# A hand-written order of steps: lead-in apart from the steady pairs, output rows scattered by halves of ranks, codes' buffers given back at the one-hots

## The reference

```python
# layer 0
h = relu(layernorm(x)); x = x + (adj / clip(adj.sum(2), 1)) @ h
# layer 1, on h = relu(layernorm(x))
neigh = (adj_ > 0) & ~eye                     # adj_: adj with ones on the diagonal
rank = cumsum(neigh) - neigh; nb = neigh.sum(-1)
skip = where(nb > 10, (nb + 1) // 2, 1)
rem = neigh & (skip > 1) & (rank % skip == skip - 1) & mask
rem = rem | rem.T; nd = where(rem, 0, adj_) > 0
s = sort(where(nd, h, inf)); nv = nd.sum(2)   # over the neighbours, for each channel
agg = sum(w * interpolate(s, tau * (nv - 1)) for tau, w in ((.25, .25), (.5, .5), (.75, .25)))
x = x + (relu((h + agg) @ W1 + b1) @ W2 + b2) * mask
```

## Time and profile before

| | us |
|---|---|
| median of 3 runs | 1654.02 |
| lowest and highest | 1653.05, 1656.76 |
| profiled execution, own time | 1666.68 |
| its span in the trace | 1664.6 |

### The profile page before, as it was taken

One profiled execution on the slowest core, in us unless ns is written; L12 is line 12 of the kernel. 1 busy time (PEld: TensorE's weight loads), 2 busy tenths in 40 slices (PEclk: granted clock), 3 DMA queues, 4 the chain that ended last, 5 costly groups with the idle time before them and its releaser, 6 DMA issues. The chain is left out here.

```text
span 1664.6 us, 29516 instructions
## 1 busy us (share of the span) xinstructions
PE 1270.5 (76%) x10929; PEld 847.7 (51%) x10929; DVE 1375.1 (83%) x2557; ACT 1227.5 (74%) x2099; POOL 775.7 (47%) x996
## 2 busy tenths in 40 slices
PE   4675897879888788878888788869888797768642
PEld 3553664556546564556546464556546564444320
DVE  3444459999899898989899898989899898969990
ACT  3687797988788797968788788868788787833310
POOL 0252425271628643383728643383616744631344
PEclk9966598999898898979898998979798898979775
DMA  5464754463536362554536363454526462330100
GB/s 157 139 208 133 235 189 138 149 205 118 171 106 219 113 219 88 172 167 136 182 104 220 112 216 94 163 164 131 197 82 224 124 210 67 109 82 23 30 12 13
DMA packets 139386, 233.99 MB, mean 141 GB/s; under 512 B 62910, under 2 KB 63438, under 8 KB 139224
## 3 DMA queue, kind: packets, MB, share of 16 engines
q1 hardware_dynamic: 124888, 185.54, 36.4%
q0 software_dynamic: 14336, 46.42, 7.4%
HBM read 181.31 MB, written 50.59 MB: 139 GB/s over the span
## 5 line engine op out<-in xcount | busy, mean ns | idle before, releaser
L560 PE MATMUL psG<-OHB,HL 128*64 128x384 f16 (+5 forms) x3584 | 387.4, 361 | 55.1 <-DVE OHB L1065 34.8
L1045 DVE TENSOR_TENSOR_SCAN VR<-NEI 128x1024 f16<-128x1024 f16 x128 | 296.8, 2336 | 125.0 <-POOL NEI L1270 57.3
L481 PE MATMUL psL<-H0A,ADJT 128*128 128x65 f32 x2048 | 311.9, 311 | 65.1 <-DMA ADJT<-in_adjt 37.3
L481 PEld LDWEIGHTS psL<-H0A,ADJT 128*128 128x128 f32 x2048 | 294.7, 224 | 101.7 <-DMA ADJT<-in_adjt 61.2
L560 PEld LDWEIGHTS psG<-OHB,HL 128*64 128x64 f16 x3584 | 213.0, 117 | 195.7 <-DVE OHB L1065 54.0
L1270 POOL TENSOR_TENSOR NEI<-NEI,CH 128x128 f16<-128x128 f16 x128 | 114.1, 894 | 295.8 <-ACT NEI L743 294.5
L1328 POOL DMA_INDIRECT rows<-VR,IDX x128 | 185.4, 1449 | 57.9 <-ACT NEI L779 34.4
L774 ACT ACTIVATE VR<-psT,CF 128x512 f16<-128x512 f32 x256 | 168.5, 681 | 24.6 <-PE psT L511 22.4
L1132 DVE TENSOR_TENSOR HUB<-HUB 128x1472 f32<-128x1472 f32 (+6 forms) x224 | 178.4, 796 | 8.1 <-ACT HUB L884 7.9
L1133 DVE TENSOR_TENSOR HUB<-HUB 128x1472 f32<-128x1472 f32 (+6 forms) x224 | 184.8, 825 | 0.0
L1362 POOL DMA_INDIRECT out<-FR x128 | 162.1, 1266 | 37.5 <-issue 36.9
(11 more groups left out here) (120 smaller groups left out, 2260.9 us busy)
## 6 DMA issues: line engine op xcount, KB each, us to landing
ADJ<-in_adj SPq DMA_DIRECT2D x128, 512.0 KB
...
RR<-rows SPq DMA_DIRECT2D x128, 288.0 KB
...
rows<-VR,IDX POOLq DMA_INDIRECT x128
out<-FR POOLq DMA_INDIRECT x128
```

The source lines that it names most:

```text
L481: m = e.matmul(ps["L"][:, 65 * (t % 4):65 * (t % 4) + 65], ADJT[:, hf, j, :], H0A[:, T * b + k, :], start=(k == 0), stop=(k == T - 1), ski ...
L560: m = e.matmul(bk[C * b:C * b + C, 0:cols], HL[:, part, (2 * g + b) % 3, k, :], OHB[:, n % 2, b, kk * cols:kk * cols + cols], start=(k == ...
L1045: e.tensor_tensor_scan(VR[:, t, 0:N], NEI[:, t, 2:N + 2], NEI[:, t, 1:N + 1], 0.0, ALU.add, ALU.add).then_inc(v_cum, 1)
```

## The change

1. The string ORDER is another one of the same letters, and the lead-in, up to the first full period, is written out in a string of its own, LEAD_IN. SKEW and LEAD go; LATE says by how many places six strands start later. The steps are the same ones, each as often; their order differs a little on every engine.
2. `out` is cut otherwise: not one graph's eight tiles after both additions, but four tiles of either graph after the addition of their half (`put`).
3. ACT's copy into POSA or POSB waits until the last one-hots of the block that used the buffer are made (DVE), instead of until they are gathered (PE).

```diff
@@ -22,19 +22,18 @@
 BIG = 1.0e9
 NOMATCH = 9999.0
 COLS = 512
-LEAD = 4
-
 
 ORDER = (
-    "mRJAssMtQQcNtfJtsQdtFMJtmQtQtdtANetdtQNQQQkmmMMQQdSdQQmQSQaQQmQQcQeLdAMMsFcmssQfQSFSALMdQcDDLMsesSAcdRmS"
-    "FMMAVessMMDDTmcSAsQEsDcEdhVSmvFKDMMKdABEBKvdBBmMDMDTdKeFEmRBmeoBEKErBldmrgNFBdKLdrrmFEmrNdeekmdmKdedXEmr"
-    "NrrmeLnQKFstnscssFKAnMsFtMcSsKLFtLScSssdAMtQsscDMdtsDcsSFEAtmMSLMcsAsMSdMEDtEcssSRcSFFADmMMFFtQTtLdFALMM"
-    "FmmAeLQFDFQLtdOMMBFFAmFFDBDQQtLdMLFeFmhBrDrFQTMtQtrlBLFFFQQetQrLdBBBBdrtgrrrGOQtmmFsJsGtdctQJsset")
-
-SKEW = {
-    "A": 24, "B": 24, "D": 24, "E": -11, "F": 13, "G": 0, "J": -3, "K": 0, "L": 7, "M": 48, "N": 6, "O": -2,
-    "Q": -24, "R": 5, "S": 16, "T": 6, "V": 0, "X": 2, "a": -1, "c": 17, "d": 3, "e": 1, "f": 0, "g": 3,
-    "h": 2, "k": 2, "l": 2, "m": 2, "n": 6, "o": 0, "r": 24, "s": 36, "t": -10, "v": 0}
+    "rrtLmJmfQFetJQsstcdJssRtmAssQQNtMJtcFdtJsMmtQtQAtdtNtdtVeQQQkMmQmQQMNQQQcdQmQedQQmdSQQQSSdAMsLFcmSQaMQfs"
+    "AMFDsLMecssDDAmdseSQhcRSFMMsmEAVDLcMTEsMAdEsSBcmKlvDFMMSKAdFDKdDDvmrTMdBBMRtFerEmBKgBBedmmBBKEELdLdemNFK"
+    "rEXmedkNmodrmrdrEmKdFFLrNermsenKsnscsscKntFsKcAtLdMsSMstssSQEcFsDtSAmcdFStMLMsscSEAMsDdMAtMDsscMFSFSmDAT"
+    "cSQERMFFMtQLtAFMDFBMmdLemFLFQQtFOFAMMDdmLAFFBQQLLtdDDBtFFTmLehFQMQrtlFrFQQtBFQteOddBgBBBtGMQrGrrr")
+LEAD_IN = (
+    "XAnnnMMAMMDDAMMADMMADRMMDTAMMBBADMrMrADDMBMTBBrBRrBrBgNrrrNsscssAsscMcNssMAkMMSScAMSMssSAMDDssccMsSSRADD"
+    "TMsMAssMcDDcMSASMMADDThBBBrrBMMlBRgBBNBXNkNnrrrrrrsnssscssccnAMMssAcMMSSsDsLAMsMScsASsDsScchMMsDSsRSDcST"
+    "AMMAMMADFLFMBBFMLFDALFFrLMBFFrBFDLDlFTFFBBBBdrdMrrrg")
+
+LATE = {"E": 11, "J": 5, "O": 2, "Q": 25, "a": 1, "t": 13}
 
 
 
@@ -136,7 +135,7 @@
 
 def strands():
 
-    s = {c: [] for c in SKEW}
+    s = {c: [] for c in ORDER}
 
     def add(c, kind, *args):
         s[c].append((kind, *args))
@@ -202,8 +201,8 @@
         for ch in range(2):
             add("E", "yt", g, ch)
             add("E", "mk", g, ch)
-        for b in range(2):
-            add("O", "out", g, b)
+        for ch in range(2):
+            add("O", "out", g, ch)
 
     for g in range(NP):
         add("X", "lx", g)
@@ -233,11 +232,12 @@
 
 def plan():
 
+
     pl = Plan()
     pl.do("start")
     steps = strands()
-    at = {c: SKEW[c] - LEAD * len(steps[c]) // NP for c in SKEW}
-    for c in ORDER * (NP + 2 * LEAD):
+    at = {c: 0 if c in LEAD_IN else -LATE.get(c, 0) for c in steps}
+    for c in LEAD_IN + ORDER * (NP + 2):
         if 0 <= at[c] < len(steps[c]):
             kind, *a = steps[c][at[c]]
             if kind in ("pos", "turn", "dg", "sc", "nvt", "nvr", "flg", "f1", "f2"):
@@ -383,6 +383,9 @@
 
             return sum(1 for s in steps[:steps.index(step)] if s[0] == kind)
 
+
+        MADE = {(g, blk): 1 + max(nth["gd", g, c, 1] for c in OF[blk]) for g in range(NP) for blk in OF}
+        LAST = {"b1": (1, "b2a"), "hub": (1, "b2b"), "b2a": (0, "b1"), "b2b": (0, "hub")}
         GATHERED = {(g, blk): 1 + max(nth["gm", g, c, 1] for c in OF[blk]) for g in range(NP) for blk in OF}
         ROWED = {g: 1 + max(nth[s] for s in steps if s[0] == "cr" and s[1] == g) for g in range(NP)}
         SUMMED = {(s[1], s[2]): 1 + i for i, s in enumerate(s for s in steps if s[0] == "wz" and s[2] != "hub")}
@@ -783,10 +786,10 @@
                 u = t_use("pos", g, b, rt)
                 blk, = [n for n, (_, r0, width) in BLOCKS.items() if r0 <= rt * P < r0 + width]
                 area, r0, _ = BLOCKS[blk]
-                before = {"b1": (g - 1, "b2a"), "hub": (g - 1, "b2b"), "b2a": (g, "b1"), "b2b": (g, "hub")}[blk]
+                back, last = LAST[blk]
                 w.wait_ge(t_full, u + 1)
-                if before[0] >= 0:
-                    w.wait_ge(p_gm, GATHERED[before])
+                if g >= back:
+                    w.wait_ge(v_oh, MADE[g - back, last])
                 e.activation(POS[area][:, b, :, rt * P - r0:rt * P - r0 + P],
                              t_bank(u).bitcast(F16).rearrange("p (k n) -> p k n", n=P), ACT.Copy).then_inc(t_empty, 1)
 
@@ -1354,10 +1357,10 @@
                 e.tensor_tensor(x1, x1, HID[:, ch, :].rearrange("p (t b c) -> p b t c", b=2, c=C), ALU.add).then_inc(
                     o_fin, 1)
 
-            def put(g, b):
-                fr = FR[:, (2 * g + b) % 4]
-                w.wait_ge(o_fin, 2 * (g + 1))
-                for rt in range(T):
+            def put(g, ch):
+                w.wait_ge(o_fin, 2 * g + ch + 1)
+                for b, rt in itertools.product(range(2), range(4 * ch, 4 * ch + 4)):
+                    fr = FR[:, (2 * g + b) % 4]
                     dst = fr[:, rt, R_DST - R_X1:R_DST - R_X1 + 2].bitcast(I32)
                     e.indirect_dma_start(out_d, bass.IndirectOffsetOnAxis(ap=dst, axis=0),
                                          fr[:, rt, 0:2 * C].bitcast(F32), None).then_inc(d_out[g % 2], 16)
```

## The result

The changed kernel takes 1704.65 us (median of four runs, 1698.42 to 1711.24) against 1654.18 us: a ratio of 1.0303, 95% interval 1.0258 to 1.0349. It is 50 us slower where 9 us faster was forecast. Run once more, beside the experiments, it gave 1.0279 (1.0222 to 1.0335). Its profiled execution reports 1711.24 us.

A forecast was written before the change was run, and what follows sets the result against it. DVE sets the pace and only its idle time, about 16 us a pair, can be won. Terms -20.1 - 5.0 - 3.8 - 4.2 + 3.0 + 21.0 = -9.1 took 1654.0 to 1645 us; range 1626 to 1666.

The forecast's parts named there:

- A: Valid-neighbour count dgv earlier on POOL: PE's 4.80 us wait and DVE's one-hot wait at chunk 7 go; -20.1 us.
- B: First half of output scatters one mask earlier on POOL: count waits of 6.5 become 0.3 and 4.4 to 6.1; -5 us.
- C: Merge step 17: its copy on ACT no longer stands behind other work; 0.95 us in four pairs, -3.8 us.
- E: adj(4,0,0) later on ACT, behind two more codes, delaying the scatter cnt(4,0,0) awaits; +3.0 us in six pairs.
- F: Short DVE waits like one of 0.69 us vanish when DVE itself comes later; -0.7 in six pairs, -4.2 us.
- D: FR's load ahead of adj(4,1,0) on SP: late ADJ tile makes DVE's merge step 20 wait 4.2 us; +21 us.
- the two other edits: Output scatters by halves, and codes' buffers freed at the one-hots instead of the gathers: both forecast at 0.
- Third rival: Slower: FR's load is late and POOL doesn't run ahead, merge step 20 waits 8 us; 1664 us, chance 0.20.

The follow-up runs named there:

- a_ov: Changed kernel with only ov(g) put ahead of res(g+2,1,0), on DVE and ACT; ratio 1.0230 to the kernel before.
- a_res: Changed kernel with only res(g+2,1,0) put ahead of cnt(g+2,1,2), on DVE and POOL; ratio 1.0145 to the kernel before.
- b_half: Kernel before with scatters out(g,0) ahead of adj(g+3,0,6) on POOL and cnt(g+3,0,6) behind one-hots gd(g+1,13,1) on DVE; ratio 1.0040.
- b_B: b_half with, on POOL, thin(g+3,0,0) also ahead of sca(g+2,1,7), mk(g,1) and res(g+3,0,0); ratio 1.0061 to the kernel before.
- b_pool: Kernel before with POOL's order alone changed: thin(g+3,0,0) ahead of sca(g+2,1,7), mk(g,1) and res(g+3,0,0); ratio 1.0006.
- b_all: Kernel before with dgv earlier, FR's load ahead of adj(.,1,0)'s loads, the moves of b_B, and ov directly behind res; ratio 1.0238.
- a_split: Changed kernel with res ahead of cnt(.,1,2), FR's load back behind adj(.,1,0)'s loads, and scatters out(g,0) split four ahead of adj(.,0,6), four behind adj(.,0,7); ratio 1.0036.
- b_split: Kernel before with dgv earlier and scatters out(g,0) split on POOL, four ahead of adj(g+3,0,7) and four behind; ratio 0.9853, twice.

## Why the prediction was wrong

In us, ratios taken times 1654:

| step | forecast | made alone | in the changed kernel |
|---|---|---|---|
| A, dgv | -20.1 | -14 | wait at gd(.,7,.) 3.1 to 0.1 or 0.9 a pair |
| B, scatters and counts | -5.0 | +10 | 6.5 to 10.1 a pair |
| C, merge 17 | -3.8 | | 0.9 to 0 or 0.4 a pair |
| E, adj(.,0,0) | +3.0 | | cnt(.,0,0) 1.6 to 0 a pair |
| F, like the 0.69 us | -4.2 | | cnt(.,1,7) 0.5 to 0.5 a pair |
| D, load of FR | +21.0 | +22 | merge 20: 0 to 4.1 or 3.2 a pair |
| ov behind res | none | +18 | 0.1 to 3.1 or 3.0 a pair |
| res late | none | +14 (a_ov less a_res) | cnt(.,1,6) 0 to 3.1 a pair |
| the two other edits | 0 | -1 | |
| lead-in | 0, -4 to +4 | | red(0) at 415.8 to 423.4 in nine traces with the new one, 408.6 to 414.3 in eleven with the old: means 419.9 and 411.0 |

**Right.** DVE bounds it and only its idle time moved. A's wait went and the gather behind it took 1.92 us; A was worth 14 us, 0.7 of the term, since cnt(.,0,0) and cnt(.,1,6) took up 1.4 us a pair of the 3.1. D stood where it was put, SP, ACT and merge step in turn, with 22 us for 21. The two edits were nothing. The small terms were not right: C had nothing to win (0.0 in the ten other traces with the old order), F's waits stayed, and E's went where +3 was forecast; none of the three was made alone.

**Wrong, B.** The step that failed is "POOL runs ahead, since mk(1,0) comes three places earlier". I looked at where one addition moved to and not at all that stands between thin(.,0,0) and adj(.,0,5). POOL's chain from adj(.,0,4) on is full (the earlier trace rows show the scatters without a gap, and the prediction said so), and the change put sca, mk and res, 3.1 us that lay in POOL's idle time before, into it. The waits of 0.3 and 4.4 to 6.1 us that I got for POOL running ahead were 1.8 and 6.4 with the scatters and cnt(.,0,6) moved alone (b_half, +7 us), where POOL is not ahead, 3.8 and 6.4 with the three instructions as well (b_B, +10 us), and 4.9 and 5.1 in the changed kernel, +3.6 us a pair. The forecast was -5, the bound +2. That the three instructions hold up cnt(.,0,5) is shown (b_pool, 1.7 to 3.8 us); that they cost time by themselves is not (1.0006).

**Wrong, what was left out.** "Most steps move by fewer than ten places" and "Four moves touch a gap" are the step that lost most. I looked for moves that touch a gap of the old trace. `ov` moved up by one place in DVE's list and `res` down by two, and they touched none: the gap at `ov` was 0.07 us, because two counts and a sum of 5.4 us lay ahead of it. The change took that cover away. This is the sum's missing term: +18 us alone. The kernel before had shown the price in a place where I did not look for it: `ov` of pair 7 in the tail, 2.9 us, behind a sum of 0.29 us that had itself waited for DVE's reductions. The late `res` is the other missing term, 14 us; its path is not shown.

**Third rival.** It named the load of FR with POOL not running ahead, and gave 1664. The load of FR cost what the forecast said; POOL not running ahead cost at the counts. The sum for D took POOL and DVE to come 5.6 us earlier both. Neither did, and what DVE waits is the difference, so that the term came out right without its premise, in part by luck. (With DVE alone ahead the same numbers give 771.6 - 761.7 = 9.9 us, not the 8 to 9 that the forecast has.)

**The sum again.** A, B, D and `ov` give 1.0215 as a product and 1.0238 together; the changed kernel has 1.0279 to 1.0303. The intervals overlap; the 7 to 11 us between are about the 9 us by which the lead-ins differ, but that attribution is only by size. The cause in the lead-in was not found, and the 14 us of the late `res`, which b_all does not have, would have to lie in those 7 to 11 us too. They do not fit beside the 9 us, nor do the 30 us between a_split and b_split: what the rest of the new order costs stays open.
